# A convolution and expert layer: product tree on VectorE, norm statistics on ScalarE, four instruction orders and one weight order rearranged

## The reference, cut to what matters

```python
x = x + tanh(g_xattn) * conv_mixer(layernorm(x), k, skip, ctx, ctx)   # v = layernorm(x)
x = x + tanh(g_ffn) * experts(layernorm(x), router_w, gate_w, up_w, down_w)

def conv_mixer(v, k, bias, x1, x2):          # D = 256 = 32 heads x 8, L = 512, batch 8
    kv  = v[:, :, :, None, :] * x2[:, :, None, :, :]        # 8 x 8 products a head
    y   = causal_convolution(kv, k)[..., :L] + kv * bias
    return einsum('bhijl,bhil->bhjl', y, x1)                # sum over i
def experts(h, ...):                          # 2048 rows of 512, 8 experts, each row to its best
    y = down[e] @ (silu(gate[e] @ h) * (up[e] @ h))
```

## Time and profile before

| | us |
|---|---|
| median of 3 runs (lowest to highest) | 666.86 (665.35 to 667.31) |
| the profiled execution's own time | 666.57 |
| its span, first to last instruction | 664.8 |
| TensorE busy | 637.8 |
| VectorE busy | 514.2 |
| ScalarE busy | 244.9 |
| GpSimd busy | 550.8 |
| TensorE's mean granted clock | 0.996 of full speed |

### The profile page before, as it was taken

How to read it: one execution, slowest core, us unless ns; L and a number is a source line. 1 busy time by engine, 2 the same in 40 slices (tenths; PEclk the granted TensorE clock), 3 DMA queues, 4 the chain that set the end, 5 groups by cost and what they waited for, 6 DMA issues and landing times.

```text
span 664.8 us, 11025 instructions
## 1 busy us (share of the span) xinstructions
PE 637.8 (96%) x3203; PEld 529.5 (80%) x3204; DVE 514.2 (77%) x651; ACT 244.9 (37%) x354; POOL 550.8 (83%) x354
## 2 busy tenths in 40 slices
PE   7998999999999999979999799999999999999995
PEld 7787888888888887868788588888888888888874
DVE  6878888888889888898799957799999938550601
ACT  5544433444443334344543133323332332333320
POOL 2999999999999999976198768788898878786852
PEclk9999999999999999999999999999999999999998
DMA  7435666666666665477676656366766644441110
GB/s 217 137 122 172 204 208 207 207 207 207 203 199 178 199 193 148 143 283 274 193 244 214 224 177 200 121 217 215 235 211 219 227 142 162 157 157 47 47 50 18
DMA packets 52642, 119.39 MB, mean 180 GB/s; under 512 B 5868, under 2 KB 6060, under 8 KB 52624
## 3 DMA queue, kind: packets, MB, share of 16 engines
q1 hardware_dynamic: 44464, 101.30, 47.5%
q0 software_dynamic: 4320, 12.72, 5.3%
q10 hardware_dynamic: 3840, 5.15, 2.8%
HBM read 94.08 MB, written 26.64 MB: 182 GB/s over the span
## 4 chain that ended last, share of the span: by engine, by line
PE 74%; DVE 15%; issue 5%; POOL 3%; ACT 1%; DMA 1%; DVEq 0%; ACTq 0%; POOLq 0%
PE pair L1527 25%; PE bank L1416 24%; PE bank L1543 13%; PE pair L1450 3%; DVE prod L1210 3%; PE pair L1386 2%; PE bank L1558 2%; DVE kv L1142 2%; DVE up L1323 1%; PE bank L1510 1%; DVE up L1320 1%; PE pair L1427 1%; POOL kv_lo L751 1%; PE bank L1500 1%; DVE gate L1320 1%
## 5 line engine op out<-in xcount | busy, mean ns | idle before, releaser
L1416 PE MATMUL bank<-kv_hi,strip 128*128 128x512 f32 x640 | 210.5, 398 | 0.1
L751 POOL TENSOR_TENSOR kv_lo<-kv,kv_hi 128x2048 fp32r<-128x2048 f32 x30 | 138.6, 4619 | 4.7 <-issue 3.8
L1416 PEld LDWEIGHTS bank<-kv_hi,strip 128*128 128x128 f32 x640 | 120.2, 188 | 25.3 <-issue 1.1
L1416 PE MATMUL bank<-kv_lo,strip 128*128 128x512 f32 x320 | 124.6, 389 | 0.0
L1178 DVE TENSOR_TENSOR prod<-bank,cT 128x512 f32<-128x512 f32 x128 | 84.8, 683 | 19.9 <-PE bank L1416 19.8
L929 ACT ACTIVATE kv_hi<-kv 128x2048 fp32r<-128x2048 f32 x30 | 57.6, 1920 | 109.8 <-DVE kv L1142 85.2
L1527 PE MATMUL pair<-gate,xT_hi 128*128 x288 | 90.8, 396 | 0.8 <-DVE xT_lo L1340 0.6
L1527 PE MATMUL pair<-up,xT_hi 128*128 (+1 forms) x288 | 88.7, 389 | 0.6 <-issue 0.6
L1416 PEld LDWEIGHTS bank<-kv_lo,strip 128*128 128x128 f32 x320 | 60.3, 188 | 11.3
L1142 DVE TENSOR_TENSOR kv<-pair,cK 128x2048 f32<-128x2048 f32 x30 | 68.4, 2280 | 0.0
L775 POOL TENSOR_TENSOR prod<-prod 128x2048 f32<-128x2048 f32 x14 | 64.5, 4605 | 0.0
(11 more groups left out here) (197 smaller groups left out, 1171.2 us busy)
## 6 DMA issues: line engine op xcount, KB each, us to landing
raw<-gate_w SPq DMA_DIRECT2D x32, 512.0 KB, 3.8
raw<-down_w SPq DMA_DIRECT2D x32, 512.0 KB, 3.8
strip<-kparts SPq DMA_DIRECT2D x15, 1024.0 KB, 6.0
raw<-up_w SPq DMA_DIRECT2D x28, 512.0 KB, 3.7
sorted_x<-fill SPq DMA_DIRECT2D x12, 1056.0 KB, 5.4
xs<-sorted_x ACTq DMA_DIRECT2D x19, 256.5 KB
x_in<-x_back SPq DMA_DIRECT2D x16, 256.0 KB, 5.4
cK<-ctx_back SPq DMA_DIRECT2D x16, 256.0 KB, 5.5
```

Of the source, the lines that this page charges most:

```text
L751: nc.gpsimd.tensor_tensor(kv_lo[u][:, hh, :], kv[:, hh, :], kv_hi[u][:, hh, :].bitcast(f32), ALU.subtract).then_inc(s_klo, 1)
L1416: last = nc.tensor.matmul(y_bank[lb][:, :], strip[u][:, 2 * hh + t, d * P:(d + 1) * P], v[u][:, hh, mb * COL:(mb + 1) * COL], start=(mb == ...
```

## The change

It takes `add_pairs` from GpSimd and `add_fours` from VectorE and puts a `tree` of three additions on VectorE at the head of its stage; `sum_heads` then adds one sum and the skip term (8 transposes instead of 12). GpSimd's first step of a stage waits for the tree. For the groups 2 to 15 of the first norm and 0 to 13 of the second, mean and variance come from two ScalarE passes that accumulate along the row (`stats1`, `stats2`) and a square root with epsilon as bias; VectorE keeps the reciprocal and the shift. The orders of TensorE, VectorE, ScalarE and GpSimd are rearranged, and the load of cK runs two groups ahead. In the expert part the load and split of expert 1's down come ahead of expert 2's up, and ScalarE makes the high parts of two chunks of expert 1's up. The diff, cut to its core (lines that only pass new arguments or declare semaphores are left out):

```diff
 # SP
-                    if known(g, lambda g: 0 < g < G - 1):
-                        load_cK(g + 1, 1 - u)
+                    if known(g, lambda g: g < G - 2):
+                        load_cK(g + 2, u)
...
-                load_three(0, UP, 1)
-                with eng.Fori(1, E - 2) as q:
+                load_matrix(eng, GATE, 2, UP, 1)
+                load_matrix(eng, DOWN, 1, GATE, 2)
+                load_matrix(eng, UP, 2, DOWN, 1)
+                load_three(1, UP, 2)
+                with eng.Fori(2, E - 2) as q:
                     load_three(q, DOWN, q)
 # GpSimd: skip_first, before_conv, stage
                     wait(eng, s_skw, g - 1)
+                    if isinstance(g, int) and (g, hh) == (G - 1, 0):
+                        eng.wait_ge(s_hot, 1)
+                    elif hh == 0:
+                        wait(eng, s_tree, STEPS * (g - 1))
...
                         else:
+                            if hh == 1:
+                                skip_last(g - 1, 1 - u, n - 1 + u)
                             kv_low(g, u, hh)
-                        if isinstance(g, int) and g == 1 and hh == 0:
-                            add_half_pairs(0, 0, 0)
...
-                    if isinstance(g, int) and g == 1:
-                        add_half_pairs(0, 0, 1)
-                    elif known(g, lambda g: g >= 2):
-                        add_pairs(g - 1, 1 - u)
-                    if known(g, lambda g: g >= 1):
-                        skip_last(g - 1, 1 - u, n - 1 + u)
 # ScalarE
+                def stats1(g, u, n):
+                    act.wait_ge(s_x[u], 16 * (n + 1))
+                    act.wait_ge(s_vtr, g)
+                    act.wait_ge(s_nb1, g)
+                    nc.scalar.activation(xn[:, :], x_in[:, u, :], ACT.Identity, scale=-1.0 / L,
+                                         accum_out=nm1[:, 0:1]).then_inc(s_mean1, 1)
+                    act.wait_ge(s_mean1, g - 1)
+                    nc.scalar.activation(xn[:, :], x_in[:, u, :], ACT.Square, bias=nm1[:, 0:1],
+                                         accum_out=sq1[:, 0:1]).then_inc(s_square1, 1)
+                    act.wait_ge(s_square1, g - 1)
+                    nc.scalar.activation(sd1[:, :], sq1[:, :], ACT.Sqrt, bias=eps_t[:, 0:1], scale=1.0 / L)\
+                        .then_inc(s_sd1, 1)
...
                     if more:
                         kv_high(g + 1, 1 - u, 0)
+                    if again:
+                        stats1(g + 2, u, n + 1)
+                        if not first:
+                            norm1(g + 2, u)
                     if not choosing and known(g, lambda g: g >= 2):
                         logits_out(g - 2)
                     skip_out(g, u)
                     if more:
                         kv_high(g + 1, 1 - u, 1)
-                    if known(g, lambda g: g < G - 2):
-                        root1(g + 2)
+                    if first:
                         norm1(g + 2, u)
...
                     if before:
-                        root2(g - 1)
+                        if final:
+                            root2(g - 1)
+                        else:
+                            stats2(g - 1, 1 - u)
                         norm2(g - 1, 1 - u)
...
-                        gate_one_high_parts(range(2, CH))
+                        one_high_parts(GATE, 3, range(2, CH))
+                        one_high_parts(UP, 4, range(2))
 # VectorE
+                def ln1_last(g):
+                    dve.wait_ge(s_sd1, g + 1)
+                    wait(dve, s_xn, g)
+                    nc.vector.reciprocal(rs1[:, :], sd1[:, :]).then_inc(s_ln1, 1)
+                    dve.wait_ge(s_ln1, g + 5)
+                    nc.vector.tensor_scalar(nb1[:, :], nm1[:, 0:1], rs1[:, 0:1], 1.0, ALU.mult, ALU.mult)\
+                        .then_inc(s_nb1, 1)
...
-                def add_fours(g, u):
+                def tree(g, u):
+                    dve.wait_ge(s_p, (g + 1) * 2 * LB)
+                    nc.vector.tensor_tensor(prod[u][:, 0:4, :], prod[u][:, 0:4, :], prod[u][:, 4:8, :], ALU.add)\
+                        .then_inc(s_tree, 1)
+                    dve.wait_ge(s_tree, STEPS * g + 1)
                     nc.vector.tensor_tensor(prod[u][:, 0:2, :], prod[u][:, 0:2, :], prod[u][:, 2:4, :], ALU.add)\
-                        .then_inc(s_add2, 1)
+                        .then_inc(s_tree, 1)
+                    dve.wait_ge(s_tree, STEPS * g + 2)
+                    nc.vector.tensor_tensor(prod[u][:, 0, :], prod[u][:, 0, :], prod[u][:, 1, :], ALU.add)\
+                        .then_inc(s_tree, 1)
...
                 def last_stage(g, u, n):
+                    places_first(dve)
+                    tree(g - 1, 1 - u)
                     product(g, u, n, 0, 0)
-                    skip_sum(g, u)
-                    places_first(dve)
-                    add_fours(g - 1, 1 - u)
...
-                split_matrix(UP, 1, 4)
+                low_parts(UP, 1, 4, range(2))
+                split_matrix(UP, 1, 4, range(2, CH))
+                    if isinstance(q, int) and q == 0:
+                        dve.wait_ge(s_down, end)
+                        split_matrix(DOWN, 0, FIRST + 1)
+                        dve.wait_ge(s_up, end)
+                        split_matrix(UP, u, FIRST + 2)
+                        return
 # TensorE
-                    terms = [0, 1, 2, 3, J] if five else [0, 1, J]
+                    terms = [0, 1, 2, 3, J] if five else [0, J]
```

More of the change, by code:

```diff
@@ L726, in _ @@
                 nc.gpsimd.memset(xn_rows[:, G * (L + 1):], 0.0).then_inc(s_const, 1)
+                nc.gpsimd.memset(eps_t[:, :], EPS).then_inc(s_const, 1)
                 eng.wait_ge(s_kpart, 1)
@@ L770, in skip_last @@
                         .then_inc(s_skp, 1)
[L772 to L776, removed]
                 def add_half_pairs(g, u, hh):
@@ L959, in stage @@
                     choosing = isinstance(g, int) and g == G - 2
+                    first = isinstance(g, int) and g == 0
+                    final = isinstance(g, int) and g == G - 1
+                    again = known(g, lambda g: g < G - 2)
                     if choosing:
@@ L1227, in stage @@
                         return
-                    product(g, u, n, 0, 0)
-                    choosing = isinstance(g, int) and g == G - 2
+                    second = isinstance(g, int) and g == 1
+                    if second:
+                        product(g, u, n, 0, 0)
+                        product(g, u, n, 0, 1)
+                    if before:
+                        tree(g - 1, 1 - u)
                     if choosing:
-                        skip_sum(g, u)
+                        pick_experts(dve, 0, 0, G1)
@@ L1232, in stage @@
+                    if not second:
+                        product(g, u, n, 0, 0)
                     if first:
                         outer(1, 1, 0, 0)
-                    product(g, u, n, 0, 1)
-                    if not choosing:
-                        skip_sum(g, u)
+                    if not second:
+                        product(g, u, n, 0, 1)
+                    if first:
+                        skip_sum(0, 0)
+                    elif again:
+                        ln1_last(g + 2)
@@ L1237, in stage @@
                     if not first:
-                        outer(g + 1, 1 - u, n + u, 0)
+                        outer(g + 1, 1 - u, n + u, 1)
+                    if before and not second:
+                        residual(g - 1, 1 - u, n - 1 + u)
                     product(g, u, n, 0, 2)
-                    if known(g, lambda g: g >= 2):
-                        add_fours(g - 1, 1 - u)
-                    if choosing:
-                        pick_experts(dve, 0, 0, G1)
-                    outer(g + 1, 1 - u, n + u, 1)
+                    if first:
+                        outer(1, 1, 0, 1)
@@ L1245, in stage @@
                     product(g, u, n, 0, 3)
-                    if not choosing:
-                        ln1(g + 2, u, n + 1)
+                    if first:
+                        ln1_last(2)
                     if second:
-                        product(g, u, n, 1, 0)
-                        product(g, u, n, 1, 1)
-                    if before:
-                        residual(g - 1, 1 - u, n - 1 + u)
-                    if not second:
-                        product(g, u, n, 1, 0)
-                    if before:
-                        ln2_first(g - 1, 1 - u)
-                        ln2_last(g - 1)
@@ L1258, in stage @@
-                    if not second:
-                        product(g, u, n, 1, 1)
+                        residual(0, 0, 0)
+                    product(g, u, n, 1, 0)
+                    if not first:
+                        skip_sum(g + 1, 1 - u)
+                    product(g, u, n, 1, 1)
+                    if before:
+                        ln2_close(g - 1)
                     product(g, u, n, 1, 2)
+                    if first:
```

(3 more changed lines are left out.)

146 lines of the change are left out of this document (90 added, 56 removed).

## The result

The changed kernel takes 659.82 us (median of 4, 658.34 to 661.62) beside 667.09 for the kernel before (4 runs in turn with it): a ratio of 0.9894, 95% interval 0.9876 to 0.9912. That is 7 us faster. I had forecast 11.4 less; the time lies just inside the upper end of my range. The profiled execution took 660.36, its span is 658.4 where before's is 664.8.

What follows compares the result with a forecast made beforehand. GpSimd was taken to pace the ten loop stages, TensorE the expert part. Gains 2.2 (loop) + 0.8 (stages 0 to 3) + 0.1 (stage 14) + 2.4 (stage 15) + 5.9 (experts) = 11.4; 666.57 - 11.4 = 655.2 us, range 650.5 to 660.

Steps and rivals of the forecast that it cites:

- The loop: Ten convolution loop stages: each falls from 17.40 to 17.2 us, together a gain of 2.2 us.
- Sum: ... = 12.3. With the 4.85 behind it a stage is 17.2: Loop stage: VectorE's chain of ten terms up to block 2 takes 12.3 us, the 21 matmuls behind it 4.85.
- the wait at block 2 for product 0.2: Loop stage, second half: TensorE stalls 0.45 us in every stage at block 2, waiting for VectorE's product 0.2.
- the second rival: Loop gains nothing: waits between three engines add 0.2 to 0.4, stage 17.4 to 17.6, time 657.5 to 660 us; chance 0.13.
- What the chain rests on: Loop: tree 4.2 us, unblocked as GpSimd stands still; GpSimd 1.1 early; ScalarE's statistics passes hidden.
- The slower rival: ScalarE's statistics become the bound if Square needs another table than Sqrt: stage 19.4, time 682 us; chance 0.04.
- Stage 15: Last convolution stage: falls from 20.84 to 18.5 us, a gain of 2.4.
- Block 0 and 1 2.1: Stage 15, second half: TensorE's blocks 0 and 1 take 2.1 us.
- Stages 0 to 3: First convolution stages: a gain of 0.8 us, estimated, with bounds from 2 later to 2 earlier.
- the stall: Experts: TensorE's stall for expert 1's down, 23.59 - 17.71 = 5.9 us, goes whole.
- behind which GpSimd was busy anyway: 0, at most 1: Experts: ScalarE's two high parts of up 1 delay a Silu by 2 us, costing 0, at most 1.

Runs made afterwards that it cites:

- d1: Changed kernel plus one extra VectorE pass (sum over cT) per stage in stages 2 to 13, placed ahead of product 0.2; span 663.5 us, one execution.
- d2: Changed kernel plus the same extra VectorE pass as d1, but placed after product 1.2; span 657.9 us, one execution.
- e4: Changed kernel with products 0.2 and 0.3 moved ahead of ln1_last, outer and residual on VectorE in stages 1 to 14; 654.59 us, ratio 0.9820.
- g1: Changed kernel without GpSimd's wait for the tree (skip_first no longer waits for s_tree); 722.88 us, one execution.
- e1: Kernel before with only the convolution part of the change, the expert part left as it was; 664.51 us, ratio 0.9961.
- e3: Changed kernel with ScalarE's two high parts of expert 1's up given back to VectorE; 658.26 us, ratio 0.9864.
- h1: Changed kernel with norm 1's statistics back on VectorE, only the square root on ScalarE; 695.53 us, one execution.
- e5: e4 with products 0.0 and 0.1 also put ahead of the tree in stage 15; 652.95 us, ratio 0.9786.
- e2: Kernel before with only the expert part of the change, the convolution left as it was; 661.75 us, ratio 0.9918.
- e6: e5 plus residual ahead of outer, norm 2's statistics ahead of the second kv_high, and no high parts of up 1 on ScalarE; 647.69 us, ratio 0.9714.

## Why the prediction was right or wrong

Of the 11.4 us forecast, the spans show 6.4. Of the 5.0 that are missing 2.2 are the loop, 1.5 stage 15, 0.9 the way to ys(1) and 0.4 the first stages.

**The loop: wrong, and by the chain's sum.** The step that failed is "Sum: ... = 12.3. With the 4.85 behind it a stage is 17.2". The mechanism was right: the wait at block 2 for product 0.2 is there, 0.50 to 0.62 (0.45 forecast), d1 and d2 show that a pass costs in this chain and only there, e4 that a shorter chain gives 0.5 us a stage. The size was off: the chain measured 12.41 and 12.53, the matmuls behind it 4.90 and 4.92, the stage 17.39. Of the 0.2 a stage that I had as the gain, nothing was left; it was smaller than what ten terms read to hundredths can carry. What I called the second rival, at 0.13, is what happened by its numbers. Its reason came true only in part: it had waits between three engines add 0.2 to 0.4, and here 0.1 to 0.2 were added, most of it between steps of VectorE itself, with no wait in them. That the time still lies inside the range is owed to that rival, which the range took in. A margin of 1% on the chain, 0.12 us, would have covered half of the gain and moved that rival's chance up.

**What the chain rests on: right.** The tree 4.19 for 4.2, not blocked; the accumulating passes 1.9 for 2.0, hidden; no table load. GpSimd waits 5.3 us a stage (69.4 in 13). g1 shows that the wait put into GpSimd is what keeps the tree short. The slower rival fell, as there is no table load in the loop. The Trainium skill, *ScalarE: Activation LUTs*, section *Table sets: the hidden batching unit*, doesn't name Square among the functions that every set has; here Square and Sqrt alternate with no load.

**Stage 15: right but for the clock.** Its steps came within 0.3 (tree at 5.5 for 5.8, block 0 at 10.5 for 10.7). The step "Block 0 and 1 2.1" took 3.72 in the profiled execution, at 1.2 GHz, and V13 to V15 was 38.21; without the fall, in five other runs with the same stage 15 (e1, e3, d1, d2, g1), it is 36.6, a gain of 2.5 on before's 39.12, where 2.4 and 0.1 were forecast. What failed is that no term stood for the clock; whether it falls in an execution is luck as far as these runs show.

**Stages 0 to 3:** 0.4 for 0.8, within its bounds. Whether the fallen clock of stage 1, for which no term stood either, took the other 0.4 is open.

**Experts: right on the stall, wrong on the side.** ys(1) to the end gave 6.0 for 5.9. The step "behind which GpSimd was busy anyway: 0, at most 1" measured 0.9 here and 1.2 by e3: GpSimd was not busy but waited 1.82 for `mid` behind that Silu, and the delay went on to `xT_lo` and TensorE. I had the bound and took its wrong end.

## What to carry to other kernels

Work that leaves a bounding engine is worth no more than the distance to the next bound, and where that is a chain of ten instructions, a gain of 1% of it is not a forecast. Ask not how busy the receiving engine is but which of its instructions somebody waits for: the tree on VectorE brought nothing as placed, and 0.5 us a stage once two short products were issued ahead of three steps of 3.3 us together, and 0.9 once the residual and the second norm's statistics were issued earlier as well (tried together only). Keep GpSimd's long passes away from VectorE's additions with a wait, even one that the data don't need.

## What the runs showed of the hardware that was not expected

An idle time of TensorE can be followed by some 3 us at a granted clock of 0.50, and its length alone doesn't say so. Behind 1.29 us (after and h1, stage 15), 1.84 and 1.97 (h1) and 2.61 (e5, turns at V1) it fell; behind 1.31 (d2, stage 15), 1.87 (h1, once), 2.60 (e4, the same turns), 3.27 (before) and 3.67 (e2, both stage 15) it did not. The same stage of the same work can fall in one execution and not in the next. The price was 1.6 us in stage 15 and 1.4 in stage 2 (V1 to V2 is 20.77 in e5, 19.32 in e4); in g1 it was nearly hidden.

In the experts GpSimd's `xT_lo` is late in some executions: d2 has a tile of 19.71 (375.33 to 395.04) where its neighbours take 17.69, e2 has one of 19.71, e3 and e6 have one of 18.7 each, after none.

```profile
377.86 0.72 PE L1622 MATMUL pair<-gate,xT_hi 128*128 x2 [1.35 <-POOL xT_lo L838]
```

Why it differs between executions was not tried and stays open. This and the clock are each 1 to 2 us in 660 and come and go from run to run: e1's twelve executions lie between 662.55, at a mean clock of 0.998, and 666.47, at 0.986. So versions a few tenths of a per cent apart could not be told from each other here by their medians, while their rows could.

A ScalarE pass with an accumulator output is followed by a read of its own of 0.19, and a root with its bias from SBUF took 0.29 to 0.30 where the kernel before has 0.18 to 0.20.
